# Preparing a later mask on ScalarE ahead of the probability copies in a graph-attention kernel

## What is computed

```python
h = relu(layernorm(x))
scores = sum(q[dst] * k[src], -1) / 16 + (edge_weight @ we + be)
exp_s  = exp(scores - segment_max(scores, dst)[dst])
attn   = exp_s / segment_sum(exp_s, dst)[dst]
out    = segment_sum(v[src] * attn, dst)
y = layer_norm(h + out + h @ ws + bs);  y = layer_norm(y + ffn(y));  result = x + y
```

## Time and profile before

| what | value |
|---|---|
| median of three executions | 2336.25 us |
| span of the profiled execution | 3211.3 us |
| PE busy, PE weight loads busy | 76%, 62% of the span |
| DVE, POOL, ACT busy | 55%, 51%, 37% |
| first stage, until the first decay | 0 to 144.4 us |
| edge loop, 440 steps | 144.4 to 2956.2 us |
| last stage | 2956.2 to 3211.3 us |
| DMA moved | 311.29 MB, mean 97 GB/s |

### The profile page before, as it was taken

One profiled execution on the slowest core, in us unless ns is written; L12 is line 12 of the kernel. 1 busy time (PEld: TensorE's weight loads), 2 busy tenths in 40 slices (PEclk: granted clock), 3 DMA queues, 4 the chain that ended last, 5 costly groups with the idle time before them and its releaser, 6 DMA issues. The chain is left out here.

```text
span 3211.3 us, 68474 instructions
## 1 busy us (share of the span) xinstructions
PE 2427.3 (76%) x14747; PEld 1996.1 (62%) x14748; DVE 1767.6 (55%) x7372; ACT 1193.2 (37%) x2930; POOL 1635.5 (51%) x1828
## 2 busy tenths in 40 slices
PE   7577677777777777777777777777777777778998
PEld 5455556556555556565656566665666666657897
DVE  7454455555555545554555555555555555556787
ACT  6333333333333333333333333333333333334666
POOL 5355565555555545555554555555555445441154
PEclk8898899899899989998998999899988899999999
DMA  7233333333233323333233333332333233222222
GB/s 231 76 103 103 99 105 101 103 98 107 90 100 100 96 86 101 97 98 96 90 102 92 96 90 96 96 98 87 96 96 100 87 92 95 83 93 71 82 74 68
DMA packets 148148, 311.29 MB, mean 97 GB/s; under 512 B 33566, under 2 KB 84625, under 8 KB 148104
## 3 DMA queue, kind: packets, MB, share of 16 engines
q0 software_dynamic: 75264, 205.62, 21.5%
q1 hardware_dynamic: 54718, 90.19, 8.6%
q10 hardware_dynamic: 18122, 14.96, 1.5%
HBM read 290.21 MB, written 20.43 MB: 97 GB/s over the span
## 5 line engine op out<-in xcount | busy, mean ns | idle before, releaser
L488 POOL DMA_INDIRECT work<-h_rows,idx x1536 | 1457.3, 949 | 1339.9 <-SPq L372 956.2
L1079 PE MATMUL bank<-work 128*128 x3520 | 939.0, 412 | 24.5 <-issue 17.7
L1011 PE MATMUL bank<-q,onehot 128*128 x5304 | 804.6, 291 | 1.2 <-DVE work L832 0.7
L1079 PEld LDWEIGHTS bank<-work 128*128 128x128 f32 x3520 | 700.1, 211 | 146.8 <-issue 45.2
L886 DVE CUSTOM_DVE_ANT_0 work<-bank,work 128x512 f32<-128x512 f32 x440 | 330.5, 751 | 778.7 <-remote 476.4
L622 ACT COPY work<-bank 128x256 f32<-128x256 f32 x880 | 295.0, 376 | 1182.6 <-remote 812.8
L832 DVE SCALAR_TENSOR_TENSOR work<-bank,work 128x257 bf16<-128x257 f32 x1764 | 651.6, 425 | 143.5 <-PE bank L1011 44.2
L1017 PE MATMUL bank<-ident,work 128*128 128x128 f32 x1764 | 307.4, 302 | 500.5 <-ACT work L622 313.3
L1011 PEld LDWEIGHTS bank<-q,onehot 128*128 128x128 bf16 x5304 | 549.5, 104 | 85.4 <-issue 1.7
L1017 PEld LDWEIGHTS bank<-ident,work 128*128 128x128 f32 x1764 | 212.8, 148 | 578.0 <-ACT work L622 442.4
L1066 PE MATMUL bank<-ident,work 128*128 128x128 f32 x1760 | 283.6, 285 | 191.8 <-ACT work L619 182.8
(11 more groups left out here) (195 smaller groups left out, 1519.5 us busy)
## 6 DMA issues: line engine op xcount, KB each, us to landing
dst_words<-dst_short SPq DMA_DIRECT2D x99, 512.0 KB
work<-h_rows,idx POOLq DMA_INDIRECT x1568
bias<-h_rows ACTq DMA_DIRECT2D x56, 128.0 KB
r_rows<-bias ACTq DMA_DIRECT2D x55, 128.0 KB
work<-r_rows SPq DMA_DIRECT2D x49, 128.0 KB, 2.3
h_rows<-acc SPq DMA_DIRECT2D x12, 512.0 KB, 6.6
work<-in_x SPq DMA_DIRECT2D x12, 512.0 KB, 3.5
out<-work SPq DMA_DIRECT2D x48, 128.0 KB, 1.7
```

The costliest lines, as they stand in the source:

```text
L488: pool.indirect_dma_start(rows[:, u, j, 0:D], None, h_rows, bass.IndirectOffsetOnAxis(idx[:, half, u * J + j:u * J + j + 1], 0)).then_inc( ...
L1011: last = nc.tensor.matmul(banks[j][:, 0:D1], onehot[:, k, j, :], q3[:, bass.ds(b, 1), c, 0:D1], start=(c == 0), stop=(c == 2))
L1079: last = nc.tensor.matmul(banks[6 + k][:, 0:D1], probs[:, j, :], rows[:, bass.ds(slot, 1), j, :], start=(j == 2), stop=(j == 1))
```

## The change

In ScalarE's part of a step, `prepare(s + 2, k)` stands ahead of the two copies in place of behind them. Beside it, values that come from loaded registers are bounded with an AND and a copy into a register where before only their bounds were stated: on SP two a chunk or fewer, on DVE in every `step_at`, on all engines once ahead of the loop. PE's `step_of` is left as it is.

```diff
+        def not_below_zero(eng, loaded, min_val, max_val):
+
+            mask = (1 << max_val.bit_length()) - 1
+            return eng.snap(eng.to_reg(eng.snap(loaded) & mask), min_val=min_val, max_val=max_val)
+
         def counts(eng):
...
-            n = eng.snap(regs[0], min_val=NW, max_val=TRIPS)
+            n = not_below_zero(eng, regs[0], NW, TRIPS)
...
-                            used_up = sp.to_reg(sp.snap(regs[u], min_val=1, max_val=T + B + S) + r * TP)
+                            used_up = sp.to_reg(not_below_zero(sp, regs[u], 1, T + B + S) + r * TP)
...
                         nc.scalar.activation(probsT, masked, ACT.Exp, bias=new_max, scale=-1.0).then_inc(exp_done, 1)
+                        prepare(s + 2, k)
                         for half in (1, 0):
                             act.wait_ge(turned, s * 2 + (2 - half))
                             nc.scalar.copy(probs[:, 2 * half:2 * half + 2, :].rearrange("p j n -> p (j n)"), banks[5 - half][:, 0:2 * P]).then_inc(probs_done, 1)
-                        prepare(s + 2, k)
...
                     def step_at(v):
-                        return dve.snap(v, min_val=0, max_val=(TP + U + HALF) * BLOCKS) + r * ROUND
+                        return not_below_zero(dve, v, 0, (TP + U + HALF) * BLOCKS) + r * ROUND
```

## The result

The changed kernel takes 2532.56 us against 2336.08 us for the kernel before, a ratio of 1.084 (95% interval 1.083 to 1.086). I had forecast 2337.5 us, 2324 to 2352. It is 196 us slower, 3.6 us for each of the 55 trips, far outside the range.

What follows compares the result with a forecast made beforehand. POOL's gather issue bounds most of the loop: last gather at 2073.0, plus 8 and 255.1, gives 2336.1 us. With mask 0 and register bounds 1.5 over the 2336.25 median, the forecast was 2337.5 us, range 2324 to 2352.

Steps and rivals of the forecast that it cites:

- What bounds the kernel: Over most of the loop, POOL's issue of gathers, 1.2525 us each: 2336.1 us, against 2262 for the chain of steps.
- the 15 us by which the late chain was to exceed the gathers: Blocks from 27 on, 100 chunks, some 122 steps: profiled chain longer by 0.15 us a chunk, 15 us in all.
- the chain's trip: One loop trip bound by steps: seven steps of 28.97 us together and an eighth of 4.85, 33.82 us.
- The chain's sum: Whole run if steps alone bound it: 439 steps 1855 us, plus 144.4 ahead, 7.5 and 255.1 behind, 2262 us.
- The mask in front of the copies: ACT's 0.63 us mask ahead of the two copies in each step: hidden, cost 0, gain behind the copies 0.
- The cover: On ACT, the mask ends before PE's turn lets the copy start at 1.53 us: 0.39 us to spare.
- The bounds on registers: Extra ANDs, mainly DVE's `step_at`, 0.1 us each: hidden in ordinary steps, 0.2 us at each trip's end, 1.5 us total.
- The work of the bounds: DVE's added register work: trip's end from 4.85 to about 5.05 us, ordinary steps stay 3.95, 1.5 us in all.
- The first on the slow side: DVE's register work outgrows its cover, 0.15 us each in line 861 of every step: 2354 us, chance 0.22.
- The other two: On ACT: copy comes 0.1 us later, 2348 us, chance 0.05; or decay was held by the mask, 2324 us, chance 0.13.

Runs made afterwards that it cites:

- The kernel that fits and leaves the mask behind the copies: Changed kernel with DVE keeping each step word and chunk number (body 338 instructions, not 359), mask moved back behind the copies: 2339.60 us, ratio 1.0025.
- that kernel's twin with the move: Changed kernel, mask in front of the copies, with DVE keeping each step word and chunk number (body 338 instructions, not 359): 2338.05 us, ratio 1.0019.
- three gathers: Changed kernel with 100 extra DVE instructions ahead of the loop, issuing and awaiting three of each chunk's four gathers: 2265.77 us, ratio 0.970.
- the shifted kernel: Changed kernel, mask in front of the copies, with 100 semaphore increments on DVE ahead of everything, shifting its loop's place: 2350.15 us, ratio 1.0059.

## Why the prediction was wrong, point by point

**What bounds the kernel: right, but the sum hit by luck.** Distrusting the idle times and adding up gathers gave 2336.1 for a measured 2336. The bound and the pitch of 1.25 us are borne out. Two other terms were wrong and cancelled. The kernel that fits and leaves the mask behind the copies is nearest to the kernel before, and its trace has no stalls: its loop's first gather starts at 123.1 us, where I had taken 150.45 from the stalled trace, and from the start of its last gather to the end of the last sum it takes 31.3 us, where I had estimated 8. With 1535 x 1.2566 = 1928.9 us of gathers and 253.9 us behind the last sum, that gives its span of 2337.2.

The 31.3 us also hold the 15 us by which the late chain was to exceed the gathers, and which I then took away as not seen in the runs. Paired with its last step by the formula for the destinations, a chunk is added up about 16 us after its fourth gather starts through most of that loop (an estimate); from about the 320th of 392 chunks on this grows, to 31 us at the last. So the 15 us were about right, as is the chain's trip (33.82 us summed, 33.88 in the late trips of that kernel's twin with the move), and it is the landing and the steps behind it that take 16 us and not 8.

The chain's sum, 2262, met the 2266 of three gathers by the same kind of luck. There the first masked maximum stands at 118.3 us, where the stalled trace had the first decay at 144.4, and 439 steps take 1883 us and not 1855.

**The mask in front of the copies: right.** Taken as 0; measured 0.5 us (2350.15 against 2349.65) and -1.5 us (2338.05 against 2339.60). The cover was PE's turn, as worked out, and the copy kept its place at 1.54. Most of the loop could not have shown a price, since the gathers set its pace; the late trips, 33.88 and 33.87 us, could, and show none.

**The bounds on registers: the failed step.** I priced each AND by the time that it runs, 45 to 150 ns, and asked only which idle time covers it. Its other price, a place in DVE's loop, wasn't in the sum. 38 more instructions in the body and 10 ahead of it moved the end from 351 to 399, over 384. The price is about 3 us at each branch, plus what follows it. Busy time by stretch, the eighth step and the one after it, first in the changed kernel, then in the shifted one:

```profile
1680.20:1688.30 8.10, 6.17 (x41) 5.14 (x38) 3.31 (x16) 2.07 (x5) 6.09 (x7) 1.00 0.43 126
1688.30:1693.50 5.20, 3.46 (x19) 3.00 (x20) 3.63 (x16) 2.18 (x5) 3.78 (x4) 0.67 0.38 106
```

```profile
1572.00:1577.20 5.20, 5.20 (x38) 4.64 (x36) 3.35 (x15) 2.07 (x5) 3.98 (x5) 1.00 0.46 125
1577.20:1581.60 4.40, 3.35 (x24) 2.45 (x24) 3.34 (x15) 2.07 (x5) 3.37 (x4) 1.00 0.42 120
```

PE ran out of work during the fetch: it is busy for 6.17 of 8.10 us, where in the shifted kernel it is for all 5.20. In the next step the granted clock is 0.67, partly at its lower level (1.2 of 2.4 GHz), where it is 1.00 in the shifted kernel. That step takes 5.15 us where it takes 4.42 without the fetch, and the second 4.38 in place of 3.91 (medians over the trips). A trip takes 39.33 us on average in the changed kernel and 35.90 in the shifted one (the start of every eighth masked maximum, 55 of them). The difference to the shifted kernel is 3.43 us, less than the medians' 3.3 + 0.7 + 0.5, since trips had room under the gathers. 55 x 3.43 = 189 us, less 4 us for the 100 extra instructions (the first masked maximum comes at 119.1 in place of 115.4 us), is 185, against 182 us between the two.

One row that could have warned me was on the page before: a queue of kind instruction with 24 packets over 55 trips, which says that the loop was held whole. Its trace has the other, the 321 records of DVE from one branch to the next. How near that was to a limit only the experiments say. I had counted the ANDs but not the body.

**The work of the bounds: right in kind, small in size.** At a trip's end I had 5.05 us, measured 5.14; ordinary steps stayed at 3.95. Of the 14 us by which the shifted kernel is above the kernel before, 4 to 5 belong to the extra instructions (the first masked maximum comes 3.7 us later, the loop's first gather 5.3) and the other 9 to 10, by subtraction, to the bounds, where I had 1.5. The body that keeps its step words brings them down to 4 (ratio 1.0019).

**The rivals.** The first on the slow side named the right edit and the right engine with a price per instruction; it ended at 2354 because it, too, counted time and no places. The other two did not occur.

**Open:** why the profile of the kernel before spans 875 us more than its runs. The profiles of the changed kernel and of all eleven experiments lie within 5 us of their runs, so neither profiling as such nor gathers beside steps explain those stalls. No experiment here touched it.

## What to carry to other kernels

Before adding instructions to an unrolled loop on an engine's sequencer, count the body and its place, not only the added time: a few register instructions can cost a fetch at every branch. If a loop slows by a constant amount per trip, look at the packets of the instruction queue and at the gap behind the branch, and test it by shifting the loop with instructions that run once. Then ask the usual question, what hides each moved operation.

## What the runs showed of the hardware

- DVE's instructions come in stretches of 128, packets of 8.2 KB. A loop that touches three stretches isn't fetched again (24 to 27 packets in all); one that touches four fetches about five packets a trip (294 to 296 in all).
- The limit is one of place: the same 359 instructions take 2349.23 us when they end at place 383 and 2574.24 us when they end at 387.
- The gap at the branch is 3.04 us with 60 instructions in the fourth stretch, 3.15 and 3.37 with 15, 3.91 with 6 and 3.85 with 3 (medians), against 0.26 us or less when the loop is held. DVE goes on 1.5 to 1.65 us after the last packet has landed.
- Over the step behind a fetch PE's granted clock is 0.67, against 1.00 without one.
- Gathers of 128 rows of 1 KB follow each other every 1.25 us on POOL, 0.949 us of it busy, and bound this loop.
